# Layer norms of three batches inside attention, and a convolution that reads its scaled product from PSUM on three bank pairs

## The reference

```python
x = x + tanh(g_xattn) * xattn(ctx, layernorm(x), W_src, W_tgt, W_out, masks)   # 8 heads of 64
x = x + tanh(g_ffn)  * ffn(layernorm(x), w1, conv_w, conv_b, w2)

def act_quant(x):                              # one scale per token
    scale = 127.0 / clip(max(abs(x), axis=-1), 1e-5)
    return clip(round(x * scale), -128, 127) / scale

def ffn(x):                                    # 512 -> 2048 -> 512
    h = act_quant(x) @ ternary(w1).T
    h = depthwise_conv1d(h, conv_w, padding=1) + conv_b   # three taps over the tokens, per channel
    h = silu(h)
    return act_quant(h) @ ternary(w2).T
```

## Time and profile before

| | us |
|---|---|
| median of 3 runs (lowest, highest) | 1886.77 (1884.56, 1887.32) |
| the profiled execution | 1887.4 |
| its span, first to last instruction | 1885.6 |
| mean granted TensorE clock | 0.954 |
| busy: PE, DVE, ACT, POOL | 1671.9, 1222.5, 785.5, 728.1 |

### The profile page before, as it was taken

The page is one execution under the profiler, slowest core; times in us unless marked ns, Lnnn a source line. Parts: engine busy times, 40 slices in busy tenths (PEclk is TensorE's granted clock), DMA queues, the critical chain, the costliest instruction groups (busy, mean ns, idle before and its releaser), DMA issues.

```text
span 1885.6 us, 24412 instructions
## 1 busy us (share of the span) xinstructions
PE 1671.9 (89%) x8738; PEld 1032.4 (55%) x8738; DVE 1222.5 (65%) x2270; ACT 785.5 (42%) x797; POOL 728.1 (39%) x318
## 2 busy tenths in 40 slices
PE   6888899999998999999999999999786876877857
PEld 5666678888885544454445444544353443444434
DVE  6777645433435667656774676565659979799793
ACT  2111122222220244423442344245338777777666
POOL 1131000000000388856885787578615044051340
PEclk9999999999998999999999999999889798997988
DMA  6656456444434531214120422042030030120201
GB/s 238 226 192 211 161 196 227 170 156 156 150 112 173 176 116 58 81 44 146 58 97 28 146 75 95 2 146 80 1 113 22 1 133 0 55 78 0 89 1 45
DMA packets 104679, 200.64 MB, mean 106 GB/s; under 512 B 7568, under 2 KB 27024, under 8 KB 104592
## 3 DMA queue, kind: packets, MB, share of 16 engines
q1 hardware_dynamic: 104592, 199.49, 30.1%
HBM read 127.90 MB, written 71.57 MB: 106 GB/s over the span
## 4 chain that ended last, share of the span: by engine, by line
PE 61%; issue 18%; POOL 8%; DVE 5%; DMA 5%; ACT 1%; SPq 1%; POOLq 0%; DVEq 0%; ACTq 0%
PE ps L1355 13%; PE ps L1367 12%; PE ps L1292 10%; PE ps L1293 9%; PE ps L1294 9%; PE ps L1330 5%; DMA wraw<-in_w2T 4%; POOL h_first L704 4%; POOL acc L699 2%; POOL h_third L704 2%; PE ps L1375 1%; PE ps L1572 1%; DVE h_first L1247 1%; DVE gp L1226 1%; DVE wabs L1087 1%
## 5 line engine op out<-in xcount | busy, mean ns | idle before, releaser
L699 POOL TENSOR_TENSOR acc<-acc,pr 128x1024 f32<-128x1024 f32 x192 | 456.9, 2380 | 119.8 <-ACT pr L729 101.9
L729 ACT ACTIVATE pr<-ps,mcol 128x1024 f32<-128x1024 f32 x256 | 284.4, 1114 | 404.6 <-PE ps L1355 399.4
L962 DVE CUSTOM_DVE_ANT_0 junk<-ps,mbias 128x512 bf16<-128x512 f32 x512 | 333.2, 689 | 168.8 <-PE ps L1330 165.0
L1367 PE MATMUL ps<-pr,vv 128*64 128x512 f32 x1024 | 273.9, 618 | 0.0
L704 POOL TENSOR_TENSOR h_first<-h_first,last_tap 128x1024 f32<-128x1024 f32 x44 | 104.7, 2382 | 293.4 <-ACT last_tap L845 293.4
L680 POOL MEMSET nmt<- 128x128 f32 x1 | 0.2, 205 | 364.0 <-DVE chl L1125 364.0
L1530 PE MATMUL ps<-xiT,w1q 128*128 128x512 bf16 x512 | 124.9, 393 | 5.8 <-ACT xiT L719 4.8
L699 POOL TENSOR_TENSOR acc<-pr 128x1024 f32<-128x1024 f32 x32 | 76.8, 2400 | 131.5 <-ACT pr L729 131.5
L1330 PE MATMUL ps<-kh,qh 64*128 64x512 f32 x512 | 118.4, 451 | 9.6 <-DMA kh<-k_split 9.3
L1572 PE MATMUL ps<-w2q,hq 128*128 128x512 bf16 x512 | 120.8, 389 | 2.6 <-ACT hq L881 1.9
L1355 PE MATMUL ps<-qh,kh 64*128 64x512 f32 x512 | 115.1, 445 | 3.7 <-ACT pr L729 3.7
(11 more groups left out here) (156 smaller groups left out, 3192.3 us busy)
## 6 DMA issues: line engine op xcount, KB each, us to landing
craw<-in_ctxT SPq DMA_DIRECT2D x8, 2048.0 KB, 9.2
xa<-in_x SPq DMA_DIRECT2D x8, 1024.0 KB, 6.7
wraw<-in_w1T SPq DMA_DIRECT2D x16, 512.0 KB, 7.4
wraw<-in_w2T SPq DMA_DIRECT2D x16, 512.0 KB, 7.8
q_split<-kqh SPq DMA_DIRECT2D x32, 256.0 KB, 2.0
q_split<-kql SPq DMA_DIRECT2D x32, 256.0 KB, 2.3
base<-lna SPq DMA_DIRECT2D x8, 1024.0 KB, 9.1
k_split<-kqh SPq DMA_DIRECT2D x32, 256.0 KB, 2.1
```

Source lines behind the costliest of these rows:

```text
L699: nc.gpsimd.tensor_tensor(acc[:, blk % 2, :], first, pr[:, (8 * blk + j) % NP, :], ALU.add).then_inc(pool_acc, 1)
L729: act.activation(pr[:, u % NP, :], ps[:, 2 * (u % 2):2 * (u % 2) + 2, :].rearrange("p a t -> p (a t)"), ACT.Exp, bias=mcol[:, (u // 64) * ...
L962: dve.tensor_tensor_reduce(out=(junk1 if n < LEAD and n % 2 else junk)[:, e, :], in0=ps[:, first_bank(n) + e, :], in1=mbias[:, b % 2, kk * ...
L1367: last = pe.matmul(ps[64 * e:64 * e + 64, 6 + blk % 2, :], vv[g % 2][:, j, 64 * e:64 * e + 64], pr[:, u % NP, e * CH:(e + 1) * CH], start= ...
```

## The change

**Layer norms.** Those of batches 0, 1 and 2 are done inside attention, while the next batch's attention runs (`layer_norm(b, k)` at macro step 32(b+1)+k, on VectorE and on ScalarE), from `bx`, where x2 lies anyway. Statistics and maxima are VectorE's; ScalarE normalises, scales and rounds, 24 operations of 128x512 for a batch, and takes a square root. The integers go to DRAM (`xi_d`) and come back as `xi` before their batch. The scales `adq` are kept for each batch, so that the feed-forward part of batches 0 and 1 has only `dve_diagonal` left to do. Batch 3 keeps its layer norm in the feed-forward part of batch 2.

**The convolution.** `gp` goes. VectorE scales the product in place in PSUM (`dve_scaled`), and both ScalarE taps and VectorE's tap read it there, on three pairs of banks (`pair(j)`, banks 0 to 5). A pair is free when VectorE's tap and ScalarE's last product of its block are done. One pair of banks (6, 7) is left for the transposes. GpSimd's addition comes after VectorE's tap. Halo columns are left out by narrower operands.

**Around them.** The queries and keys of group 0 are loaded before the last chunk, and the first score tiles come later in it (`K_PART` is 10, new `V_UNITS`). The first exponential doesn't wait for the stores of keys and ternary weights; the second does. TensorE sums the last four units of the last block itself (`DIRECT`). The last projections are mixed with `ln_row`, `ln_turn` and `first(0)`, `first(1)`. w1 and w2 are loaded at the end of attention. The `Fori` over batches is unrolled.

The diff, cut to its core:

```diff
@@ the convolution's loop on TensorE
-                    if j + 3 < KH:
-                        first(j + 3)
-                    pe.wait_ge(dve_d, dn + D_DVE[f"c0{j}"])
-                    if j >= 2:
-                        pe.wait_ge(act_d, an + D_ACT[f"silu{j - 2}"])
+                    if j >= 1 and j + 2 < KH:
+                        pe_first(pe, b, j + 2)
+                    pe.wait_ge(pool_tap, b * KH + j + 1)
+                    if j >= 1:
+                        pe.wait_ge(act_d, an + D_ACT[f"silu{j - 1}"])
                     for i in range(NT):
-                        last = pe.transpose(ps[:, 4 + 2 * (j % 2) + i // 4, ...
+                        last = pe.transpose(ps[:, 6 + i // 4, ...
+        def pe_first(pe, b, j):
+            if j >= 3:
+                pe.wait_ge(dve_d, b * D_DVE_N + D_DVE[f"c0{j - 3}"])
+                pe.wait_ge(act_d, b * D_ACT_N + D_ACT[f"c2_{j - 3}"])
+            for t in range(2):
+                for k in range(KD):
+                    last = pe.matmul(ps[:, 2 * (j % 3) + t, :], w1q[:, k, j * P:(j + 1) * P], ...
+            last.then_inc(pe_h, 1)
@@ on VectorE
+        def dve_scaled(dve, b, j):
+            dve.wait_ge(pe_h, b * KH + j + 1)
+            dve.tensor_tensor(pair(j), pair(j), row[:], ALU.mult).then_inc(dve_d, 1)
                 for j in range(KH):
                     if j + 2 < KH:
-                        scaled(j + 2)
-                    dve.wait_ge(pool_tap, b * KH + j + 1)
-                    dve.scalar_tensor_tensor(out=h[j % 3], in0=gp[:, j % 3, 0:S], scalar=convw[:, j, 0:1], in1=h[j % 3],
+                        dve_scaled(dve, b, j + 2)
+                    done(f"g{j}")
+                    dve.wait_ge(act_d, an + D_ACT[f"c2_{j}"])
+                    dve.scalar_tensor_tensor(out=h[j % 3][:, 1:S], in0=pair(j)[:, 0:S - 1], scalar=convw[:, j, 0:1], in1=h[j % 3][:, 1:S],
@@ on GpSimd
                     pool.wait_ge(act_d, b * D_ACT_N + D_ACT[f"c2_{j}"])
-                    nc.gpsimd.tensor_tensor(h[j % 3], h[j % 3], last_tap[j % 2][:], ALU.add).then_inc(pool_tap, 1)
+                    pool.wait_ge(dve_d, b * D_DVE_N + D_DVE[f"c0{j}"])
+                    nc.gpsimd.tensor_tensor(h[j % 3][:, 0:S - 1], h[j % 3][:, 0:S - 1], last_tap[j % 2][:, 0:S - 1], ALU.add).then_inc(pool_tap, 1)
@@ on ScalarE
-                    act.activation(h[j % 3], gp[:, j % 3, 1:S + 1], ACT.Identity, bias=convb[:, j:j + 1],
+                    act.activation(h[j % 3], pair(j), ACT.Identity, bias=convb[:, j:j + 1],
-                    act.activation(last_tap[j % 2][:], gp[:, j % 3, 2:S + 2], ACT.Copy, scale=convw[:, j, 2:3]).then_inc(act_d, 1)
+                    act.activation(last_tap[j % 2][:, 0:S - 1], pair(j)[:, 1:S], ACT.Copy, scale=convw[:, j, 2:3]).then_inc(act_d, 1)
@@ the layer norm inside attention, VectorE (steps k of a batch)
+                if 1 <= k < 1 + NT:
+                    dve.wait_ge(dve_free5, use5["y", b, k - 1] + 1)
+                    dve.bn_stats(st2[:, k - 1, :], bx[:, k - 1, :]).then_inc(dve_lc, 1)
+                if 13 <= k < 13 + NT:
+                    i = k - 13
+                    dve.wait_ge(act_lc, b * LC_ACT_N + LC_ACT[f"n{i}"])
+                    dve.tensor_reduce(amax[:, i:i + 1], lnx[:, i, :], AX.X, ALU.max, apply_absolute_value=True).then_inc(dve_lc, 1)
@@ ... and ScalarE
+                if k == 10:
+                    act.activation(rs2[:, 0, :], mv2[:, :, 1], ACT.Sqrt, bias=eps).then_inc(act_lc, 1)
+                if 12 <= k < 12 + NT:
+                    act.activation(lnx[:, i, :], bx[:, i, :], ACT.Identity, bias=nmr[:, i:i + 1],
+                                   scale=rs2[:, 1, i:i + 1]).then_inc(act_lc, 1)
@@ SyncE, per group
+                if g % PAIRS == 2 and b:
+                    sp.wait_ge(sp_x2_out, 16 * b)
+                    sp.wait_ge(act_lc, (b - 1) * LC_ACT_N + LC_ACT[f"n{NT - 1}"])
+                    sp.wait_ge(dve_lc, (b - 1) * LC_DVE_N + LC_DVE[f"stat{NT - 1}"])
+                    sp.dma_start(bx[:], base_d[b * S:(b + 1) * S, :]...).then_inc(sp_bx, 16)
+                if g % PAIRS == 3 and b:
+                    sp.wait_ge(act_lc, b * LC_ACT_N)
+                    sp.dma_start(xi_d[(b - 1) * S:b * S, :]..., xic[:]).then_inc(sp_xi_out, 16)
@@ SyncE, before the last chunk
+                if last and not half:
+                    for sl in range(2):
+                        sp.wait_ge(sp_q_out[sl], 32 + 64 * NCH)
+                        sp.wait_ge(sp_k_out[sl], 32 + 64 * (NCH - 1))
+                    sp.wait_ge(dve_cl, NCH * KS)
+                    load_qk(0)
@@ ScalarE, start of attention
-            for sl in range(2):
-                act.wait_ge(sp_k_out[sl], 32 + 64 * NCH)
-            act.wait_ge(sp_wq_out, 16 + 32 * NCH)
+                    if s == 0 and a == 1:
+                        for sl in range(2):
+                            act.wait_ge(sp_k_out[sl], 32 + 64 * NCH)
+                        act.wait_ge(sp_wq_out, 16 + 32 * NCH)
@@ TensorE, end of attention
+            ln_row(pe, 0)
+            ln_turn(pe, 0, 0)
+            ln_turn(pe, 0, 1)
+            project(B - 1, 0)
+            ln_turn(pe, 0, 2)
+            ln_turn(pe, 0, 3)
+            project(B - 1, 1)
+            pe.wait_ge(sp_w1, 16)
+            pe.wait_ge(act_ln, LN_ACT_N)
+            pe_first(pe, 0, 0)
+            project(B - 1, 2)
+            pe_first(pe, 0, 1)
+            for i in range(3, NT):
+                project(B - 1, i)
```

More of the change, by code:

```diff
@@ L81, in flamingo_gated_block @@
         deq1 = cst[:, 11:12]
+        magic = cst[:, 12:13]
         bq = sb("bq", [P, PAIRS], F32)
@@ L665, in _, with load_x2 @@
-            store_load(B - 1)
-            store(B - 1)
-            sp.wait_ge(sp_out, 16 * B + 16)
+            def load_x2(b):
+                sp.dma_start(x2[:], x2_d[b * S:(b + 1) * S, :].rearrange("(j p) d -> p j d", p=P)).then_inc(sp_x2_in, 16)
+            load_x2(0)
+            load_xn(B - 1)
+            for b in range(B):
+                if b + 1 < B - 1:
+                    sp.wait_ge(pe_ct, (b + 1) * KH)
+                    sp.wait_ge(pool_tap, (b + 1) * KH)
+                    load_xi(b + 1)
+                sp.wait_ge(dve_d, (b + 1) * D_DVE_N)
+                sp.dma_start(out[b * S:(b + 1) * S, :].rearrange("(j p) d -> p j d", p=P), x2[:]).then_inc(sp_out, 16)
+                sp.wait_ge(sp_out, 16 * (b + 1))
+                if b + 1 < B:
+                    load_x2(b + 1)
@@ L689, in _ @@
             for blk in range(2 * NG):
-                for j in range(1, NT):
+                for j in range(1, NT if blk < LAST else NT // 2):
                     pool.wait_ge(act_p, 8 * blk + j + 1)
@@ L1186, in last_chunk @@
                 for m in range(PAIRS):
-                    dve_tops(dve, K_UNITS[m, 0])
-                    dve_tops(dve, K_UNITS[m, 1])
+                    for part in range(2):
+                        if m:
+                            dve_tops(dve, K_UNITS[m, part])
                     dve.wait_ge(pe_bk, (NCH - 1) * PAIRS + m + 1)
@@ L1198, in last_chunk @@
                 for j in range(CT):
-                    for part in range(2):
-                        if (j, part) in V_UNITS:
-                            dve_tops(dve, V_UNITS[j, part])
+                    if j == 2:
+                        dve_rows(dve, 0)
+                    for k in range(KS):
+                        if (j, k) in V_UNITS:
+                            dve_tops(dve, V_UNITS[j, k])
                     dve.wait_ge(pe_bv, (NCH - 1) * CT + 8 + j + 1)
@@ L1369, in product @@
                 last.then_inc(pe_pv, 1)
+                if u >= DIRECT:
+                    pe.wait_ge(dve_free4, use4["z", LAST])
+                    for e in range(2):
+                        pe.matmul(ps[64 * e:64 * e + 64, 4, :], ones[:, 0:HD], pr[:, u % NP, e * CH:(e + 1) * CH], start=u == DIRECT, stop=False)
             def sums(blk):
-                pe.wait_ge(pool_acc, 7 * (blk + 1))
+                pe.wait_ge(pool_acc, 7 * blk + (7 if blk < LAST else 3))
                 pe.wait_ge(dve_free4, use4["z", blk])
                 for e in range(2):
-                    last = pe.matmul(ps[64 * e:64 * e + 64, 4, :], ones[:, 0:HD], acc[:, blk % 2, e * CH:(e + 1) * CH], start=True, stop=True)
+                    last = pe.matmul(ps[64 * e:64 * e + 64, 4, :], ones[:, 0:HD], acc[:, blk % 2, e * CH:(e + 1) * CH],
+                                     start=blk < LAST, stop=True)
                 last.then_inc(pe_z, 1)
@@ L1523, in ffn @@
                 dn, an = b * D_DVE_N, b * D_ACT_N
-                def first(j):
-                    if j >= 2:
-                        pe.wait_ge(dve_d, dn + D_DVE[f"g{j - 2}"])
-                    for t in range(2):
-                        for k in range(KD):
-                            last = pe.matmul(ps[:, 2 * (j % 2) + t, :], w1q[:, k, j * P:(j + 1) * P], xiT[:, k, t * 512:(t + 1) * 512],
```

(9 more changed lines are left out.)

276 lines of the change are left out of this document (163 added, 113 removed).

## The result

The changed kernel takes 2179.2 us (median; 2177.2 to 2180.6) against 1887.05 us of the kernel before: 1.155 times the time, interval 1.153 to 1.157. The prediction said 2178 us. The profiled execution took 2177.2 us with a span of 2175.4 us; before it was 1887.4 and 1885.6.

The account below looks back on a forecast made before the run. The prediction took a ring through VectorE, GpSimd and TensorE in the convolution loop to bound the changed kernel. 1887.4 + 316 - 8 - 4 + 2 - 14 - 1 = 2178 us; own range 2135 to 2212, 2040 to 2212 with the warm ring.

Parts of the forecast that it names:

- the ring: Convolution loop: tap, GpSimd's addition, transposes, next first product, scaling, next tap run one after another; loss 316 us.
- third rival: Convolution loop: only the three bank pairs bind, 4.47 us a turn, 1873 us; chance 0.05.
- second rival: Convolution loop: VectorE's three operations bind, 3.45 us a block, 1827 us; chance 0.07.
- The price of a turn: Convolution loop: 10.25 us a block, with 5.23 from transposes to scaling; bounds 7.89 and 10.53 us.
- The bound for a clock that stays up: Convolution loop, rival: never cold, 2.87 us from transposes to scaling, 7.89 a turn, 2047 us; chance 0.08.
- The in-place write to PSUM: VectorE's scaling in the convolution: no added time taken, bounds -0.1 and +0.2 us each.
- A batch's stage: Feed-forward, first(0) to the reduction of all maxima: 154.2 us against mean 75.2, 79 us lost per batch.
- the early load: Start of attention: group 0's queries and keys loaded earlier and used later gain 8 us, bounds 5 and 11.
- the exponential: Start of attention: first exponential no longer waits for the ternary weights' store; gain 4 us, bounds 2 and 5.
- The layer norm inside attention: Attention, three batches: added layer-norm work lies beside TensorE; loss 2 us, bounds 0 and 8.
- The end of attention: Between attention and feed-forward: layer norm and `ul` wait go, clock improves; gain 14 us, bounds 8 and 18.
- The second halves: Second half of batches 0 and 1, without the next layer norm on VectorE: gain 1 us, bounds 0 and 2.

Follow-up runs that it names:

- e5: Changed kernel with GpSimd's addition done twice per block, first into a scratch tile nobody reads: 2315.5 us.
- e4: Changed kernel with 16 unread filler matmuls per block on TensorE, before its wait for GpSimd's addition: 2080.4 us.
- e1: Changed kernel with TensorE's first product of block j+3 put ahead of the transposes of block j, as in the kernel before: 1887.6 us.
- e3: Changed kernel with both queue edits, TensorE's first product ahead of the transposes and VectorE's tap ahead of the scaling: 1823.5 us, 0.967 of the kernel before.
- e2: Changed kernel with VectorE's tap of block j ahead of its scaling of j+2, TensorE's order as changed: 1918.6 us.
- e8: Changed kernel with group 0's queries and keys loaded late again, behind the last but one half chunk: 2187.4 us.
- e9: Changed kernel with the first exponential, not the second, waiting again for the last stores of keys and ternary weights: 2182.0 us.
- e6: Changed kernel with three short layer-norm steps on ScalarE instead of VectorE and the clamp of the maxima left out for batches 0 to 2: 2169.3 us.

## Why the prediction was right, point by point

**What bounds the kernel, and the ring.** Right, and shown. The ring has the members that the prediction names, in that order, and two experiments change its length alone: e5 by GpSimd's operation, e4 by the clock. Opening it where the rivals did (first(j+2) off T(j-1)) gives the third rival's pace, 4.41 us in e1 (4.47 was written). The second rival's pace, 3.45 us as written, comes in e3 alone, which has VectorE's order changed too; the prediction gave TensorE's order as its only condition, and with that alone the three bank pairs bind. The ring needs both orders: e1 takes away TensorE's, which is new, e2 VectorE's, which the kernel before has as well, and that gives back 292 and 261 us. Whether GpSimd's addition ahead of the tap, as before, would have opened the ring wasn't tried.

One row is misread in the prediction. The matmuls at 1653.52 are those of first(4), not of first(3), which lie among the 32 at 1640.39. The banks of first(4) came free when the scaling at 1645.78 ended, at 1647.01, so what the row was to show stands: TensorE doesn't start later matmuls while earlier transposes wait.

**The price of a turn.** 10.25 us was written. The first batch has 10.30 us in nearly all its turns; the others begin at 9.1 to 9.3 us and settle at 10.24, with a mean of 10.09 (10.06 in the last). From transposes to scaling 5.23 us was written, from four batch starts, and 5.33 us is measured at 1647.91, 5.25 on average over the 52 turns. The bound for a clock that stays up, 2.87 us, is 2.86 us in e4. The in-place write to PSUM, taken at nothing with bounds of -0.1 and +0.2 us, costs nothing: 1.23 us a scaling against 1.21 to 1.23.

**A batch's stage.** 154.2 us was written from first(0) to the reduction of the maxima; the second batch takes 152.1 us (1578.12 to 1730.18), and the last 151.6. From scaling(2) on, where the four batches can be compared, the stages grew from 70.1, 70.1, 68.9 and 70.0 us to 149.4, 146.7, 146.7 and 146.3 us: 310 us in place of 316. The shorter first turns are the difference.

**The start of attention.** 8 us were written for the early load with its later first use, and 4 us for the exponential, 12 in all. From TensorE's first matmul of the last chunk to the first block's sums it is 98.0 us where it was 108.4: a gain of 10.4 us. Its parts are less sure than the sum. The trace of e8 gives the early load alone 1.4 us, and that of e9 gives the exponential's later wait 0.25 us. So the step that gave 4 us to this wait isn't borne out, and most of the 10.4 us belongs to what neither run takes back: the later first use of the scores and the moved stores. TensorE's wait in the last chunk is now for VectorE, as the prediction said of the part that stays:

```profile
575.95 0.79 PE L1427 MATMUL ps<-kh,qh 64*128 64x512 f32 x2 [4.78 <-DVE nmv L1019]
```

In the profiled pair, the first block's sums come 15.6 us sooner than before (673.76 to 658.17). That isn't a gain of 15.6 us: 5.2 of it lie ahead of the last chunk, which begins anywhere from 558.8 to 567.4 us over eight profiled kernels whose code is the same up to there (560.2 in the changed kernel, 565.4 before).

**The layer norm inside attention.** This term was mis-sized: 2 us written, bounds 0 and 8, measured 13.2. The step that failed is "all lies beside TensorE", with small operations on VectorE counted as small. The large operations do lie beside it: with the short steps that stay, they cost the 2 us that e6 leaves. The short steps that e6 moves or leaves out cost 11.2 us, because each `tensor_scalar` that meets an addition of GpSimd waits for its end, and the score maxima in VectorE's queue stand behind it. Their slack is small: VectorE's idle gaps in that stretch are some 0.6 us (before the maxima at 927.95 it waits 0.59 us for TensorE). The prediction had looked at the two-input operations alone. Yet the kernel before shows a `tensor_scalar` being held too, at the end of attention:

```profile
1341.30 13.20 DVE L923 TENSOR_SCALAR xn<-xn,mv,rs 128x512 f32<-128x512 f32 x8
...
1337.97 14.87 POOL L699 TENSOR_TENSOR acc<-acc,pr 128x1024 f32<-128x1024 f32 x6
...
1485.71 3.74 DVE L923 TENSOR_SCALAR xn<-xn,mv,rs 128x512 f32<-128x512 f32 x8
```

Eight of them take 13.20 us there, and 3.74 us where GpSimd is idle: the five that meet an addition take 1.84 to 2.60 us each, the three behind the last one 0.53. The Trainium skill, "SBUF — State Buffer", section "Who interferes with whom", also lists `tensor_scalar` among the operations that can take the port pair shared with GpSimd, and says that `tensor_reduce` never does; the traces agree, with 2.38 us for eight columns, and 0.68 us for a maximum over 512 columns at 916.66, in the middle of an addition (915.30 to 917.70). The prediction used the sentence on two inputs from that section and passed over this one.

**The end of attention.** 14 us written, 16.6 measured: from the 31st block's sums to scaling(2) it is 44.4 us where it was 61.0. The wait for `ul` is gone and the clock is 1.00:

```profile
1348.35 1.03 PE L1476 MATMUL ps<-acc,ones 128*64 128x512 f32 x4
...
1380.88 1.89 PE L1534 MATMUL ps<-xiT,w1q 128*128 128x512 bf16 x8 [0.94 <-DVE bx L1070]
```

**The second halves** gain 1.1 us in all; 1 was written. Together: 1887.4 + 309.9 - 15.6 + 13.2 - 16.6 - 1.1 = 2177.2 us, the profiled execution's time. The loop came out 6 us shorter than written and the three gains 6 us larger (5.2 of them by where the last chunk happened to begin), and the attention stage 11 us longer: the closeness of 2178 to 2179 owes something to errors that cancel. The ring's 310 us doesn't.

## What to carry to other kernels

- Before counting what a change takes off an engine, write down for each queue which instruction stands behind which, and follow one block around: if the chain comes back to its start through three engines with nothing beside it, its length is the time of a turn, and no engine's busy share shows it. Here one line of queue order decided between 2179 and 1888 us, and a second one between 1888 and 1823 us; the second alone gives 1919 (e2).
- In this ring TensorE's idle stretch (4.9 us a turn) is paid twice: once as waiting and once, 2.5 us, at half clock behind it.
- A run that takes one part of a change back is read in its trace too, from a point where the code is still the same: the medians gave e8 8.2 us and the stretch that it touches 1.4.
- A short operation isn't cheap by its size when it can be held by a long one of another engine; look in the trace for the same kind of operation beside that engine's work.
